# Second and fourth pass of a four-stage image kernel: normalisation factors copied to all channels by transfers instead of products

## What is computed

```python
def _ln(x, g, b):
    m = jnp.mean(x, axis=-1, keepdims=True)
    v = jnp.var(x, axis=-1, keepdims=True)
    return (x - m) * jax.lax.rsqrt(v + EPS) * g + b
...
h = _ln(x, g1, b1)                       # over the 96 channels of a pixel
...                                      # windows of 7 x 7 pixels
qkv = (h @ w_qkv + b_qkv).reshape(-1, N, 3, nh, hd)
attn = softmax(jnp.einsum('wqhd,wkhd->whqk', q, k) * scale)
out = jnp.einsum('whqk,wkhd->wqhd', attn, v).reshape(-1, N, C)
x = shortcut + (out @ w_proj + b_proj)
h2 = _ln(x, g2, b2)
return x + gelu(h2 @ w_fc1 + b_fc1) @ w_fc2 + b_fc2
```

## Time and profile before

| | us |
|---|---|
| median of 3 runs | 11,815.78 (11,811.32 to 11,822.69) |
| profiled execution, its own time | 11,807.14 |
| its span | 11,805.3 |
| TensorE busy | 11,116.6 (94%) |
| ACT busy | 7,831.3 (66%) |
| VectorE busy | 7,378.2 (62%) |
| POOL busy | 5,227.8 (44%) |

### The profile page before, as it was taken

One profiled execution on the slowest core, in us unless ns is written; L12 is line 12 of the kernel. 1 busy time (PEld: TensorE's weight loads), 2 busy tenths in 40 slices (PEclk: granted clock), 3 DMA queues, 4 the chain that ended last, 5 costly groups with the idle time before them and its releaser, 6 DMA issues. The chain is left out here.

```text
span 11805.3 us, 397033 instructions
## 1 busy us (share of the span) xinstructions
PE 11116.6 (94%) x158740; PEld 8317.4 (70%) x158740; DVE 7378.2 (62%) x12642; ACT 7831.3 (66%) x13524; POOL 5227.8 (44%) x6916
## 2 busy tenths in 40 slices
PE   6999999899999999998989999998999999999999
PEld 2444444577777777777767777776888888788887
DVE  4444444577777777775447777776666666666665
ACT  4555555477777777776337777775777777777776
POOL 0000000377777777775014544443555555555554
PEclk9999999899999999999989999998999999999999
DMA  1111111122222222222643333332010000010100
GB/s 54 39 40 36 40 35 40 33 53 50 52 51 51 51 52 51 51 51 77 216 146 80 81 79 79 80 79 54 24 25 24 25 24 24 25 25 25 24 24 22
DMA packets 1105622, 617.63 MB, mean 52 GB/s; under 512 B 864651, under 2 KB 1076566, under 8 KB 1099704
## 3 DMA queue, kind: packets, MB, share of 16 engines
q1 hardware_dynamic: 1091496, 553.66, 19.3%
q10 hardware_dynamic: 12288, 38.54, 1.0%
HBM read 308.38 MB, written 282.75 MB: 50 GB/s over the span
## 5 line engine op out<-in xcount | busy, mean ns | idle before, releaser
L1484 POOL TENSOR_TENSOR L_HdL<-L_Hd,L_HdH 128x392 fp32r<-128x392 f32 x1536 | 1572.7, 1024 | 283.8 <-POOL L_HdH L1482 283.1
L1468 POOL TENSOR_TENSOR L_SQ<-L_X 96x392 f32<-96x392 f32 x512 | 428.5, 837 | 2298.8 <-DMA L_X<-after_L 2288.6
L991 PE MATMUL banks<-L_ident,L_PR 113*113 113x113 f32 x9216 | 1201.1, 267 | 1.2 <-DVE L_X L1390 0.7
L991 PEld LDWEIGHTS banks<-L_ident,L_PR 113*113 113x113 f32 x9216 | 1143.1, 180 | 63.8 <-DVE L_X L1390 9.8
L1219 ACT COPY L_PT<-banks 113x452 f32<-113x452 f32 x1792 | 885.8, 538 | 371.1 <-PE banks L991 369.2
L1235 ACT ACTIVATE L_PR<-L_SX 113x588 f32<-113x588 f32 x1536 | 1088.0, 708 | 52.3 <-DVE L_SX L1362 10.3
L1482 POOL CAST L_HdH<-L_Hd 128x392 fp32r<-128x392 f32 x1536 | 785.1, 511 | 740.5 <-issue 658.1
L395 PE MATMUL banks<-scan_XS,scan_W1T 97*96 (+1 forms) x2688 | 1111.4, 552 | 0.0
L1054 PE MATMUL banks<-L_VB,L_PT 113*49 113x34 f32 x36864 | 1064.1, 213 | 2.0 <-ACT L_PT L1219 1.0
L1262 ACT ACT_TABLE_LOAD x512 | 656.9, 1283 | 607.3 <-PE banks L998 607.2
L1356 DVE TENSOR_REDUCE L_MX<-banks 113x12 f32<-113x588 f32 x1024 | 783.4, 765 | 432.2 <-PE banks L1037 432.2
(11 more groups left out here) (239 smaller groups left out, 27006.6 us busy)
## 6 DMA issues: line engine op xcount, KB each, us to landing
L_X<-after_L SPq DMA_DIRECT2D x768, 147.0 KB
after_L<-L_X SPq DMA_DIRECT2D x512, 147.0 KB
conv_T<-L_norm_by_phase SPq DMA_DIRECT2D x96, 512.0 KB, 3.3
L_norm_by_phase<-L_XP SPq DMA_DIRECT2D x512, 84.0 KB, 2.1
scan_XT<-in_x SPq DMA_DIRECT2D x33, 1176.0 KB, 7.1
L_norm<-L_XA SPq DMA_DIRECT2D x256, 147.0 KB, 1.9
L_conv<-conv_D ACTq DMA_DIRECT2D x96, 392.0 KB, 3.0
L_XR<-L_norm SPq DMA_DIRECT2D x256, 147.0 KB, 2.6
```

Of the source, the lines that this page charges most:

```text
L991: mm = pe.transpose(bank(TURN[a])[0:SPAN, (k % 4) * SPAN:(k % 4 + 1) * SPAN], PR[:, st.v if lag else st.u, 2 * k:2 * k + 2, :].rearrange(" ...
L1484: pool.tensor_tensor(HdL[:, u, j].bitcast(F32R), Hd[:, u, j], HdH[:, u, j], ALU.subtract).then_inc(s[f"hd_parts_{j}"], 1)
```

## The change

`spread` and `PICK` go. There is a new tile `RB` in SBUF with the factors on 96 partitions, double buffered. After it has written `RS`, ACT waits for that and issues one transfer a group: the first row of the group, read 96 times, into `RB`. VectorE waits for the transfer of each group just ahead of the product that needs it, and reads `RB` in place of PSUM. Since banks 0 to 2 are no longer written by `spread`, the waits of `variances` and `scores` on `xn`, `xh` become waits on `lv`; ACT waits before it writes `RS` until the older buffers were used.

```diff
@@ names and buffers
-            J = sb("J", [C, NORM_ROWS]); PICK = sb("PICK", [C, C])
+            J = sb("J", [C, NORM_ROWS]); RB = sb("RB", [C, 3 if kind == "L1" else 2, 2, CH])
...
+        spread_rows = [[sem(f"spread{g}{u}") for u in range(2)] for g in range(3 if kind == "L1" else 2)] if mlp else []
@@ TensorE, variances
-                    if kind == "L1":
-                        st.wait("xh", 5)
-                    else:
+                    st.wait("lv", 0)
+                    if kind == "L3":
                         st.wait("y", 4)
@@ TensorE
-                def spread(st):
-
-                    st.wait("rstd", -1)
-                    for k in range(PAIRS):
-                        cols = slice(2 * TOK * k, 2 * TOK * (k + 1))
-                        for g, _ in norms(st):
-                            rows = slice(NORM_ROWS * g, NORM_ROWS * (g + 1))
-                            mm = pe.matmul(bank(NORM_BANK[g])[0:C, cols], PICK[rows], RS[rows, st.u, cols], start=True, stop=True)
-                    mm.then_inc(s["spread"], 1)
@@ TensorE, scores
-                        if st.ahead().f:
-                            st.wait("xn", -1)
-                        if third_norm(st):
-                            st.wait("xh", 4)
+                        st.wait("lv", -1)
@@ TensorE, mlp_step
-                    if normed:
-                        spread(st)
...
                     if st.n and kind == "L3":
+                        if normed:
+                            st.wait("lv", -1)
@@ ACT, rstd
                     st.wait("lv", -1)
+                    for g in present:
+
+                        st.wait(("xn", "xn2", "xh")[g], (1, 4, 6)[g])
                     for rows in parts:
                         ins = act.activation(RS[rows, st.u], LV[rows, st.u], ACT.Exp, scale=-0.5)
                     ins.then_inc(s["rstd"], 1)
+                    st.wait("rstd", -1)
+                    for g in present:
+                        act.dma_start(RB[:, g, st.u], RS[NORM_ROWS * g:NORM_ROWS * g + 1, st.u].unsqueeze(1).broadcast_to([1, C, CH])).then_inc(spread_rows[g][st.u], 16)
@@ VectorE, normalised
-                    st.wait("spread", -1)
                     if st.m:
-                        dve.tensor_tensor(XN2[0:C, st.u], x1_of(st, 2)[0:C], bank(NORM_BANK[1])[0:C, 0:CH], ALU.mult).then_inc(s["xn2"], 1)
+                        st.wait_turn(spread_rows[1][st.u], 2, 1)
+                        dve.tensor_tensor(XN2[0:C, st.u], x1_of(st, 2)[0:C], RB[:, 1, st.u], ALU.mult).then_inc(s["xn2"], 1)
...
-                        dve.tensor_tensor(XH[:, st.u], X2[0:C, st.u], bank(NORM_BANK[2])[0:C, 0:CH], ALU.mult).then_inc(s["xh"], 1)
+                        st.wait_turn(spread_rows[2][st.u], 4, 1)
+                        dve.tensor_tensor(XH[:, st.u], X2[0:C, st.u], RB[:, 2, st.u], ALU.mult).then_inc(s["xh"], 1)
```

More of the change, by code:

```diff
@@ L778, in window_pass @@
             loads += [(gb[:, 0:1], column(p["dw_b"]))]
-        load_all(nc, kind, loads, zeros=zeros, values=[(J[:], 1.0 / C), (PICK[:], 0.0)] if mlp else [])
+        load_all(nc, kind, loads, zeros=zeros, values=[(J[:], 1.0 / C)] if mlp else [])
         with nc.Block() as block:
@@ L787, in _ @@
                     dve.memset(eps[:], EPS)
-                    for g in range(C // NORM_ROWS):
-                        dve.memset(PICK[NORM_ROWS * g:NORM_ROWS * g + 1], 1.0)
                 if kind == "L3":
@@ L828, in window_pass @@
             names += ["xn_high", "xn_parts", "xn2_high", "xn2_parts"]
-            names += ["sq", "sq2", "variances", "lv", "rstd", "spread", "xn2", "fc2", "x2"]
+            names += ["sq", "sq2", "variances", "lv", "rstd", "xn2", "fc2", "x2"]
             names += [f"fc1_{j}" for j in range(HB)] + [f"gelu_{j}" for j in range(HB)]
@@ L852, in window_pass @@
         K_BANK, Q_BANK = (7, 3) if mlp else (3, 6)
-        VAR_BANK, NORM_BANK = 2, (0, 1, 2)
+        VAR_BANK = 2
         TOKEN_BANK = (2, 6)
@@ L1195, in _ @@
                     variances(first)
-                    spread(first)
                 over_chunks(pe, s, mlp_step if mlp else attention_step, LAST)
@@ L1397, in normalised @@
                     nx = st.ahead()
-                    st.wait("spread", -1)
                     if st.m:
-                        dve.tensor_tensor(XN2[0:C, st.u], x1_of(st, 2)[0:C], bank(NORM_BANK[1])[0:C, 0:CH], ALU.mult).then_inc(s["xn2"], 1)
+                        st.wait_turn(spread_rows[1][st.u], 2, 1)
+                        dve.tensor_tensor(XN2[0:C, st.u], x1_of(st, 2)[0:C], RB[:, 1, st.u], ALU.mult).then_inc(s["xn2"], 1)
                     if nx.f:
                         nx.wait_turn(loaded[nx.of4(0)], 0, N_LOADS, 4)
-                        dve.tensor_tensor(seen(XN[0:C, nx.u]), win(X[0:C, nx.of4(0)]), win(bank(NORM_BANK[0])[0:C, 0:CH]), ALU.mult).then_inc(s["xn"], 1)
+                        nx.wait_turn(spread_rows[0][st.u], 0, 1)
+                        dve.tensor_tensor(seen(XN[0:C, nx.u]), win(X[0:C, nx.of4(0)]), win(RB[:, 0, st.u]), ALU.mult).then_inc(s["xn"], 1)
                     if st.m:
```

## The result

| | us |
|---|---|
| before, median of 4 runs | 11,818.98 (11,811.32 to 11,822.69) |
| after, median of 4 runs | 19,020.53 (19,014.08 to 19,023.11) |
| ratio | 1.610, interval 1.608 to 1.612 |
| profiled execution, its own time | 19,014.08 |
| its span | 19,012.3 |

The kernel became 61% slower, as forecast: 19,020 against 19,550, inside the range of 18,000 to 21,200. The 7,202 us are 28.1 us for each pair of steps, one of the second and one of the fourth pass.

The account below looks back on a forecast made before the run. A closed loop from L_RS through VectorE, TensorE and POOL was taken to bound the second pass, with 1.3 us slack in the fourth. 256 x 17.6 + 256 x 12.7 = 7,757 us on 11,807 gave 19,550, range 18,000 to 21,200.

Parts of the forecast that it names:

- Bound, and who waits: Second pass: closed loop L_RS, VectorE, TensorE, POOL with almost no slack; fourth pass: 1.3 us slack before the hidden block.
- P, 6.0 us per transfer: Moving part of each new one-partition transfer, at 25 GB/s: 6.0 us, own range 5.3 to 6.9, besides 1.25 us fixed.
- Source doesn't matter: Rival, chance 0.14: new transfers move at 230 GB/s, the second lands at 2.6 us, time 12,170 us.
- The third transfer, 19.35: Second pass: transfers follow one another in one queue, so VectorE stands at XH until 19.35 us instead of 2.95.
- Overlap: Rival, chance 0.08: the third transfer lands with the second, second pass costs 4.4 us less a step, time 18,430 us.
- The PT copies: ACT's three issues, 1.0 us, delay the PT copies and heads by less than 1 us, covered by the transfer wait.
- The clock, 1.9 us in both passes: TensorE's pauses drop the granted clock to 0.50 once a step, costing 1.9 us a step in both passes.
- The rival "Clock": Chance 0.10: all as forecast, but TensorE keeps 2.4 GHz; 512 x 1.9 us less, time 18,580 us.
- The bound of +2,600 us: Upper end of the clock term over both passes, if the clock never rises in TensorE's critical stretch.
- The removed products: Twelve products a step in the second pass, eight in the fourth: 0.86 us each step, 440 us if TensorE never waited.
- Faster: Rival, chance 0.04: TensorE bounds, 440 us gained, time 11,370; needs second landing within 1.3 us, 2.5 in the fourth pass.
- the signs asked for: Later profile: landings 7, 13, 19 us; VectorE idle about 10 and 5; TensorE near 45%; steps near 30 and 26.5.

## Why the prediction was right, and where its terms were off

**Bound, and who waits.** Right. The closed loop through L_RS, VectorE, heads and TensorE in the second pass, and the slack of 1.3 us in the fourth, gave the lengths: L1046 moved by 13.56 us, the fourth pass's hidden block by 14.38 - 4.33 = 10.05, against 16.2 and 10.8.

**P, 6.0 us per transfer.** Right in kind, a little high. In the fourth pass XN2 stands at 12.61 after L_RS: with 0.05 and the fixed 1.25 that leaves 5.65 for each of the two, 26.6 GB/s instead of 25; the window with 28 GB/s says the same. The row that carried it was the one small transfer out of one partition. The run with 32 source rows showed that it is the source: 12.7 us to landing against 3.0. This rules out "Source doesn't matter". That the engines are "not full" when one partition feeds them, as I read from their 18% in the earlier trace rows, did not hold here: they were busy 89% at 28 GB/s. The Trainium skill (SBUF — State Buffer, Door 1: The DMA port swizzle) has 27.2 GB/s for the partitions behind one port, by which a transfer takes 5.5 us; it comes nearer than my 25, and the trace of the fourth pass agrees with it within 3%.

**The third transfer, 19.35.** Wrong, by 2.7 us a step, some 700 us in all. This is the term of the sum that was mis-sized. It was built on transfers that follow one another because they share a queue. They don't: XH stood at 16.62, the third transfer ran beside the second, and with partition 32 as its source, 18.96. So the rival "Overlap" had the right mechanism and 2.7 of its 4.4 us: it expected XH 1.62 after XN2, and XH came 3.3 after. And the gain was not free: with three transfers in the second pass XN2 comes 0.7 later than with two in the fourth (13.33 and 12.61).

**The PT copies.** The size was wrong, the conclusion held. The first two issues take 0.6 us each, the third up to 6.96 (the row of the issue, 515/615/6959), and ACT stands in it. The copies come 8.1 us late, not 1, and the heads on TensorE with them. The heads end at 4014.3, though, and VectorE asks for them only after XH at 4019.3, so the wait for the transfers covers it all. In the step shown of the run with 32 source rows the 2 us were covered too, by the wait for XN2L; what they did there was to add the pause behind which the clock fell.

**The clock, 1.9 us in both passes.** The mechanism was right and the total near (1,100 us against 973), the split wrong: 3.2 to 3.5 in the fourth pass and 1.1 in the second. In the fourth, 9 of the 13 us between hidden and L_RS ran at 0.50 (hidden to L_RS took 12.97 us against 9.43 in the earlier trace rows); I had supposed that part of the stretch sees the full clock again sooner. In the second, the critical stretch begins only at L1046, TensorE has by then worked since 4017.8, and from 4026 on its products are at full speed again; L1046 to the next L_RS takes 8.45 us against 7.34, which holds the 0.5 that I had taken off for POOL, too. The rival "Clock" is ruled out by the granted clock of 0.62 and 0.69, and by both runs with filling products. The bound of +2,600 us for a clock that never rises was added up wrong: it counts the whole 4 and 6 us, of which 1.9 each are in the forecast already, so it should be about +1,600.

**The removed products.** I took the same 0.86 us for eight as for twelve products, and this was right for a reason that I did not have: groups run side by side. As a gain it appears nowhere, as the prediction said of the second pass. The rival "Faster" fell short at its own condition in the second pass, a landing within 1.3 us. In the fourth the best source and order came near its 2.5 and was still 0.4% slower than the kernel before: at that point the chain of XN2 sets the start of the hidden block, and the time of the removed products is waited away.

**The sum.** By steps: second pass 27.5 - 13.0 = 14.5 us against 17.6, fourth 27.5 - 13.9 = 13.6 against 12.7. By the two timelines the errors are -2.64 us for the third transfer, -0.3 from L1046 to L_RS in the second pass (1.11 against 1.9 - 0.5), -0.75 for P in the fourth and +1.64 for the clock there (3.54 against 1.9): -2.05 x 256 = -525 us, which is the difference between 19,550 and the time measured. So it is as close as it is by luck: three terms too large and one too small met. Of the signs asked for, the step of the fourth pass came out a little long (26.5 forecast, 27.5 found), that of the second short (30 forecast, 27.5 found), the first transfer landed after 7.5 us as asked and the last after 15.7 at most where 19 was asked, VectorE's wait ahead of XN2 was 12.0 instead of about 10, ahead of XH 1.57 instead of about 5, and TensorE was busy 58 and 61% instead of 45, since half speed makes its work longer.

## What to carry to other kernels

A transfer that copies one partition to many moves at a pace that its source sets, here 26.6 GB/s for 150 KB, and the busy share of the DMA engines, 89% here, doesn't tell such a transfer from a fast one; read the GB/s beside it. Where the row stands in 32 partitions already, reading all of them lands four times sooner. In this loop without slack, even the fast form costs more than the products that it replaces: count from the write of the source to the landing (2.5 us here), and compare with the slack at the consumer, not with the busy share of the engine that is relieved. Before counting a gain for removed products of 32 rows, see whether they run beside others that stay; and after any new wait of TensorE, ask which stretch behind it runs at the low clock and who waits for that stretch.

## What the runs showed of the hardware that was not expected

- The third transfer in a row held the issuing engine for up to 6.96 us where the first two took 0.6 each; with sources of 32 partitions for 2.0 at most. In the step shown it came free at 8.1 us after L_RS, about when the first transfer lands (7.5 us after its issue). Whether it waits for room in the queue or for the first transfer's end was not told apart.
- Transfers of one queue overlap: VectorE had that of partition 64 3.3 us after that of partition 32, and a third out of partition 32 delayed the second by 3.2 us. The Trainium skill (SBUF — State Buffer, "Can I just issue two DMAs to hit both halves?") states of transfers at partitions 0 and 64 that they serialize, with 6% gained. Here the measurement speaks against it for a single source partition each: 150 KB more, from partition 64, cost 3.3 us and 0.7 on the transfer ahead, where the same from one partition costs 5.65.
- TensorE's granted clock fell from 1.00 to 0.50 over a pause of 1.54 us (the windows at 3998 and 4000.91 of the first run with filling products; two shorter pauses, of 1.36 and 0.70 us, lay ahead of it), not only over those of 4 us as in the earlier trace rows. A look for long waits alone misses it.
- VectorE's product into XH, 0.56 us in the changed kernel, took 1.15 to 1.31 in the median in the two runs with other single rows (0.87 with 32 rows). Its cause stayed open; it adds up to 0.7 us a step to those runs.
